# A decoder layer on one core: cross-attention's values projected in the first-norm stage instead of the sums stage

## The reference

```python
# self-attention: h = layernorm(x), scaled, quantised to 8 bits with a power-of-two scale
#   from max |h| over everything; q, k, v = quantised h @ w_qkv; 16 heads of 64
dots = fq_floor(q @ k.T * temp)              # scale again from a maximum over everything
attn = fq_floor(softmax(dots))               # needs the maximum over every row's sum
# cross-attention of x1 (the first block's result) to ctx (8, 512, 384)
k = ctx @ Wk + bk
v = ctx @ Wv + bv                            # 16 heads of 32
x = softmax(q @ k.T * scale) @ v @ Wo + bo
```

## Time and profile before

| | us |
|---|---|
| median of 3 runs | 2945.56 |
| lowest, highest | 2941.08, 2950.68 |
| profiled execution, its own time | 2947.2 |
| its span | 2945.4 |
| mean granted TensorE clock | 0.943 of 2.4 GHz |
| busy: TensorE, VectorE, ScalarE, GpSimd | 87%, 81%, 48%, 7% |

### The profile page before, as it was taken

The page is one execution under the profiler, slowest core; times in us unless marked ns, Lnnn a source line. Parts: engine busy times, 40 slices in busy tenths (PEclk is TensorE's granted clock), DMA queues, the critical chain, the costliest instruction groups (busy, mean ns, idle before and its releaser), DMA issues.

```text
span 2945.4 us, 43234 instructions
## 1 busy us (share of the span) xinstructions
PE 2549.4 (87%) x13176; PEld 995.6 (34%) x13176; DVE 2387.9 (81%) x4130; ACT 1403.5 (48%) x2456; POOL 217.9 (7%) x210
## 2 busy tenths in 40 slices
PE   3299899969999957777769799999999999999997
PEld 3244322212222224444335222222223444444443
DVE  7889499999999969999889589988897755555554
ACT  2200233318998989999523155555555322221211
POOL 0000233310111110000000000111100000000000
PEclk7599999969998979999989899999999999999999
DMA  8342222214454543443216633443355510000000
GB/s 320 109 184 93 90 105 101 94 65 158 164 180 150 164 144 113 128 125 114 72 43 200 152 84 102 115 110 103 101 169 197 197 72 29 29 29 28 29 29 29
DMA packets 197749, 332.90 MB, mean 113 GB/s; under 512 B 32504, under 2 KB 118520, under 8 KB 187248
## 3 DMA queue, kind: packets, MB, share of 16 engines
q1 hardware_dynamic: 193312, 314.51, 33.2%
q10 hardware_dynamic: 4304, 16.78, 1.5%
HBM read 200.70 MB, written 130.51 MB: 112 GB/s over the span
## 4 chain that ended last, share of the span: by engine, by line
PE 53%; DVE 21%; issue 15%; ACT 7%; DMA 2%; DVEq 1%; SPq 0%; POOLq 0%; POOL 0%; ACTq 0%
PE bank L1068 9%; PE bank L1234 7%; PE bank L1223 7%; ACT arena L1329 6%; DVE stats L1516 6%; PE bank L1024 4%; DVE arena L1797 4%; PE bank L1032 4%; PE bank L1008 4%; PE bank L1122 3%; DVE arena L1812 3%; PE bank L915 2%; PE bank L923 1%; PE bank L1040 1%; PE bank L983 1%
## 5 line engine op out<-in xcount | busy, mean ns | idle before, releaser
L1516 DVE TENSOR_REDUCE stats<-bank 128x1024 f32 (+1 forms) x352 | 406.4, 1216 | 54.8 <-PE bank L892 32.4
L1329 ACT ACTIVATE arena<-arena 128x512 bf16<-128x512 int8 x512 | 361.4, 713 | 72.9 <-DVE arena L1733 72.8
L1750 DVE CUSTOM_DVE_ANT_0 arena<-bank,arena,fac 128x512 int8<-128x512 f32 x512 | 355.8, 740 | 20.7 <-PE bank L915 20.7
L1917 DVE TENSOR_REDUCE arena<-bank 128x2 f32<-128x1024 f32 x256 | 312.5, 1223 | 52.1 <-PE bank L1024 36.4
L1422 ACT ACTIVATE arena<-bank 128x1024 f32<-128x1024 f32 x256 | 248.0, 1022 | 189.4 <-PE bank L1040 189.4
L1354 ACT ACTIVATE arena<-arena 128x512 f32<-128x512 int8 x512 | 323.7, 774 | 14.6 <-DMA arena<-dq_scr 14.6
L1492 ACT ACTIVATE arena<-bank,bf_s,fac 128x512 f32<-128x512 f32 x128 | 99.5, 778 | 434.1 <-PE bank L1226 434.1
L1307 ACT ACTIVATE arena<-bank,floor_c,fac 128x1024 int8<-128x1024 f32 x96 | 115.6, 1204 | 355.2 <-PE bank L855 304.6
L1068 PE MATMUL bank<-arena 128*32 128x512 f32 x2048 | 270.0, 604 | 0.0
L855 PE MATMUL bank<-arena 128*128 128x512 bf16 x1024 | 245.4, 384 | 26.3 <-DMA arena<-hq_scr 13.2
L1234 PE MATMUL bank<-arena 128*128 128x512 f16 x1024 | 245.6, 379 | 7.6 <-DVE arena L2114 7.1
(11 more groups left out here) (211 smaller groups left out, 3397.3 us busy)
## 6 DMA issues: line engine op xcount, KB each, us to landing
dq_scr<-arena SPq DMA_DIRECT2D x128, 256.0 KB, 2.1
arena<-dq_scr SPq DMA_DIRECT2D x128, 256.0 KB, 2.6
arena<-half_scr SPq DMA_DIRECT2D x256, 128.0 KB, 2.8
qkv_scr<-arena SPq DMA_DIRECT2D x8, 3072.0 KB, 9.7
arena<-in_x SPq DMA_DIRECT2D x16, 1024.0 KB, 8.4
arena<-qkv_scr SPq DMA_DIRECT2D x128, 128.0 KB, 2.4
half_scr<-arena SPq DMA_DIRECT2D x32, 512.0 KB, 4.0
x_scr<-arena SPq DMA_DIRECT2D x16, 1024.0 KB, 5.7
```

Of the source, the lines that this page charges most:

```text
L1329: last = A(e_dump[:, NT * (h % 2) + t, :], dq8[:, h % 4, t, :], ACT.Exp, bias=negm_b[:, par, c:c + 1], scale=exp_scale, accum_out=sum_b[:, ...
L1516: return V.tensor_reduce(dst, src, ax, ALU.max, apply_absolute_value=True)
L1750: V.tensor_tensor_reduce(dq8[:, s, t, :], bank[:, t, :], floor_row, fac[:, C_DOTS:C_DOTS + 1], -3.0e38, ALU.add, ALU.max, accum_out=ymax[: ...
L1917: V.tensor_reduce(mxX[:, mp, hs, 2 * u:2 * u + 2], bank[:, at:at + 2, :], AX.X, ALU.max).then_inc(S("sX_red"), 1)
```

## The change

Values are projected in the first norm. TensorE's `ctx_values(b)` follows `turn_z(b)`: 12 products in four banks; ctx and values go round banks 4 to 7 with one count (`kv_bank`, seven units a batch). ScalarE copies each block to `vI`, now two buffers (`values_kept`, after `h_out(b)`), GpSimd adds the bias in place, SyncE stores it. `cx` is a single buffer; Wv and bv are loaded at the start. VectorE's loop is now first_norm(b + 1), h_peak(b). In the sums stage only keys are left, one block each 16 tiles, a third of it after tiles 2, 7 and 12; VectorE evicts blocks 0 and 2, ScalarE 1 and 3. Scores go round six banks, and VectorE's loop over batches is written out.

```diff
@@ -267,9 +268,12 @@
 w8 = cB(I8, 4096)
-cx = cB(F32, 2, NT, DC)
+Wv_s = cB(F32, CC, D)
+bv_s = cB(F32, D)
+cx = cB(F32, NT, DC)
+vI = cB(F32, 2, D)
 KEEP_AT = ARENA - (24 + 8) * 256 - NB * CC * T
-assert cB.at <= KEEP_AT
+assert cB.at <= KEEP_AT, (cB.at, KEEP_AT)
 cxT = Carve(KEEP_AT)(F32, NB * CC, T)
@@ -445,11 +447,12 @@
     for b in range(NB):
+        if b + 1 < NB:
+            sp.wait_ge(S("kv_mm"), b * UNITS_V + CC)
+            load_ctx(b + 1)
         if b + 2 < NB:
             sp.wait_ge(S("z_turned"), b * NT + NT)
             load_x(b + 2)
-            sp.wait_ge(S("kv_mm"), b * CC + CC)
-            load_ctx(b + 2)
         sp.wait_ge(S("h_ready"), b * KC + KC)
@@ -457,6 +460,10 @@
                 load_h(n)
+        for t in range(NT):
+            sp.wait_ge(S("v_ready"), b * NT + t + 1)
+            sp.dma_start(v_scr[b * KC:b * KC + KC, :, t, :].rearrange("o p c -> p o c"),
+                         vI[:, t % 2, :].rearrange("p (o c) -> p o c", o=KC)).then_inc(S(f"v_stored{t % 2}"), 16)
     for n in (0, 1):
@@ -528,11 +530,9 @@
                 load_pair(b + 1, p)
-            if p == 2 and b:
+            if p == 1 and b:
                 store_k(b - 1)
-        store_v(b)
     store_k(NB - 1)
-    sp.wait_ge(S("v_stored"), 64 * NB)
     sp.wait_ge(S("k_stored"), 32 * NB)
@@ -767,7 +767,13 @@
     over_partitions(1, S_GAMMA, S_BETA + 1)
-    over_partitions(2, S_WQKV, S_WOUT + 1)
+    pool.wait_ge(S("wI_in"), 32)
+    for b in range(NB):
+        for t in range(NT):
+            pool.wait_ge(S("kv_evac"), b * UNITS_V + CC + t + 1)
+            nc.gpsimd.tensor_tensor(vI[:, t % 2, :], vI[:, t % 2, :], bv_s, ALU.add).then_inc(S("v_ready"), 1)
+        if b == 2:
+            over_partitions(2, S_WQKV, S_WOUT + 1)
     over_partitions(3, S_H, S_H + 1)
@@ -788,8 +794,8 @@
         for o in range(KC):
-            pool.wait_ge(S("kv_evac"), NB * CC + b * KC + o + 1)
-            if o == 0 and not is_batch(b, 0):
+            pool.wait_ge(S("t32_in"), b * KC + o + 1)
+            if o == 0 and b:
                 pool.wait_ge(S("k_stored"), b * 32)
@@ -833,20 +839,36 @@
+    def kv_bank(b, n):
+        before = b * UNITS_V + n - 4
+        if before >= 0:
+            pe.wait_ge(S("kv_evac"), before + 1)
+        return bank[:, 4 + (b * UNITS_V + n) % 4, :]
     def turn_ctx(b):
-        pe.wait_ge(S(f"c_in{b % 2}"), 16 * (b // 2) + 16)
+        pe.wait_ge(S("c_in"), 16 * b + 16)
         for k in range(CC):
-            n = b * CC + k
-            if n >= 4:
-                pe.wait_ge(S("kv_evac"), n - 3)
+            dst = kv_bank(b, k)
             for t in range(NT):
-                last = nc.tensor.transpose(bank[:, 4 + n % 4, P * t:P * t + P], cx[:, b % 2, t, P * k:P * k + P], ident[:, :])
+                last = nc.tensor.transpose(dst[:, P * t:P * t + P], cx[:, t, P * k:P * k + P], ident[:, :])
+            last.then_inc(S("kv_mm"), 1)
+    def ctx_values(b):
+        pe.wait_ge(S("kv_evac"), b * UNITS_V + CC)
+        for t in range(NT):
+            dst = kv_bank(b, CC + t)
+            for k in range(CC):
+                last = mm(dst, cxT[:, b * CC + k, P * t:P * t + P], Wv_s[:, k, :], start=k == 0, stop=k == CC - 1)
             last.then_inc(S("kv_mm"), 1)
     for b in range(NB):
         turn_ctx(b)
         turn_z(b)
+        if b == 0:
+            pe.wait_ge(S("wI_in"), 32)
+        ctx_values(b)
     pe.wait_ge(S("h_ready"), NB * KC)
-    pe.wait_ge(S("kv_evac"), NB * CC)
+    pe.wait_ge(S("kv_evac"), NB * UNITS_V)
@@ -914,18 +936,11 @@
-    def kv_step(b, p, k):
+    def key_step(b, o, k):
+        if k == 0 and b * KC + o >= 2:
+            pe.wait_ge(S("t32_in"), b * KC + o - 1)
+        last = mm(bank[:, 6 + o % 2, :], Wk_s[:, k, P * o:P * o + P], cxT[:, b * CC + k, :],
+                  start=k == 0, stop=k == CC - 1)
         if k == CC - 1:
@@ -934,11 +949,11 @@
             for t in range(NT):
-                pe.wait_ge(S("dq_done"), b * (H * NT) + NT * h + t + 1 + 4)
-                scores(h, t, bank[:, t, :]).then_inc(S("rs_tile"), 1)
-                n = NT * (h % 2) + t
-                if n in (1, 4, 7):
-                    kv_step(b, h // 2, n // 3)
+                n = b * (H * NT) + NT * h + t
+                pe.wait_ge(S("dq_done"), n + 3)
+                scores(h, t, bank[:, n % 6, :]).then_inc(S("rs_tile"), 1)
+                if n % 16 in (2, 7, 12):
+                    key_step(b, h // 4, n % 16 // 5)
     barrier(pe, 6)
@@ -1289,14 +1304,24 @@
     def ctx_turned_out(b):
-        for n in range(b * CC, b * CC + CC):
+        for k in range(CC):
+            n = b * UNITS_V + k
             act.wait_ge(S("kv_mm"), n + 1)
-            A(cxT[:, n, :], bank[:, 4 + n % 4, :], ACT.Copy).then_inc(S("kv_evac"), 1)
+            A(cxT[:, b * CC + k, :], bank[:, 4 + n % 4, :], ACT.Copy).then_inc(S("kv_evac"), 1)
+    def values_kept(b):
+        for t in range(NT):
+            n = b * UNITS_V + CC + t
+            act.wait_ge(S("kv_mm"), n + 1)
+            if b * NT + t >= 2:
+                act.wait_ge(S(f"v_stored{t % 2}"), 16 * (b * NT // 2 + t // 2))
+            A(vI[:, t % 2, :], bank[:, 4 + n % 4, :], ACT.Copy).then_inc(S("kv_evac"), 1)
     for b in range(NB):
         ctx_turned_out(b)
         if b == 0:
             act.wait_ge(S("b16_ready"), 1)
         h_out(b)
+        values_kept(b)
     barrier(act, 3)
@@ -1329,7 +1354,7 @@
             last.then_inc(S("sum_done"), 1)
-            if h % 4 == 3:
+            if h % 8 == 7:
                 keys_kept(b, h // 4)
@@ -1640,8 +1665,8 @@
     for b in range(NB - 1):
+        first_norm(b + 1)
         h_peak(b)
-        first_norm(b + 1)
         if b == 2:
@@ -1733,11 +1758,12 @@
-    def values_kept(b, t):
-        dve.wait_ge(S("kv_mm"), NB * CC + b * PAIRS + 2 * t + 1)
-        if t == 0 and not is_batch(b, 0):
-            dve.wait_ge(S("v_stored"), b * 64)
-        V.tensor_tensor(vI[:, t, :], bank[:, 4 + t % 2, :], bv_s, ALU.add).then_inc(S("v_ready"), 1)
+    def keys_kept(b, o):
+        dve.wait_ge(S("kv_mm"), NB * UNITS_V + b * KC + o + 1)
+        if b:
+            dve.wait_ge(S("split_done"), b * KC + o + 1 - KC)
+        V.tensor_scalar(t32[:, o, :], bank[:, 6 + o % 2, :], HALF, bk16[:, o:o + 1], ALU.mult, ALU.add
+                        ).then_inc(S("t32_in"), 1)
@@ -1747,7 +1773,7 @@
                 hold(dve)
-                V.tensor_tensor_reduce(dq8[:, s, t, :], bank[:, t, :], floor_row,
+                V.tensor_tensor_reduce(dq8[:, s, t, :], bank[:, (b * (H * NT) + NT * h + t) % 6, :], floor_row,
                                        fac[:, C_DOTS:C_DOTS + 1], -3.0e38, ALU.add, ALU.max,
@@ -1755,16 +1781,18 @@
                         pair_max(b - 1, 1 - par, PAIRS - 1, t)
-                if h % 4 == 3 and t == 0:
-                    values_kept(b, h // 4)
+                if h % 8 == 4 and t == 0:
+                    keys_kept(b, h // 4 - 1)
             if h == 5 and not is_batch(b, 0):
                 keep_rows(b - 1, 1 - par)
     dve.wait_ge(S("wI_in"), 16 * 4)
     V.tensor_scalar(bk16, bk16, HALF, None, ALU.mult).then_inc(S("b16_ready"), 1)
+    dve.wait_ge(S("b16_ready"), 2)
     dve.wait_ge(S("part_sized"), NB)
     link(amax(peak[:, S_WFC:S_WPROJ + 1], w_peak[:, :].rearrange("p (w n) -> p w n", w=2)))
     dve.sem_inc(peak_ready, 1)
-    through(dve, quantise)
+    for b in range(NB):
+        quantise(b, b % 2)
     for step in (0, 1):
         pair_max(NB - 1, 1, PAIRS - 1, step)
     dve.wait_ge(apeak_ready, 6)
```

More of the change, by code:

```diff
@@ L40 @@
 DUOS = QKV_UNITS // 2
+UNITS_V = CC + NT
 NEXT_AT = (7, 9, 11, 13)
@@ L100, in sem @@
             return ctx.enter_context(nc.semaphore(name))
-        ARENA = 196 * 1024 // 4
+        ARENA = 198 * 1024 // 4
         arena = sb("arena", [P, ARENA], F32)
@@ L432, in load_ctx @@
             def load_ctx(b):
-                sp.dma_start(cx[:, b % 2], tok(ctx_768[b])).then_inc(S(f"c_in{b % 2}"), 16)
+                sp.dma_start(cx, tok(ctx_768[b])).then_inc(S("c_in"), 16)
             load_ctx(0)
+            sp.dma_start(Wv_s, chunk(Wv)).then_inc(S("wI_in"), 16)
             load_x(0)
             load_x(1)
-            load_ctx(1)
+            sp.dma_start(bv_s, bv.rearrange("(a n) -> a n", a=1).broadcast_to([P, D])).then_inc(S("wI_in"), 16)
             def load_h(b):
@@ L479, in _ @@
             sp.wait_ge(S("hq_stored1"), 16 + 16 * NB // 2)
+            for n in (0, 1):
+                sp.wait_ge(S(f"v_stored{n}"), 32 * NB)
             barrier(sp, 3)
-            sp.dma_start(Wv_s, chunk(Wv)).then_inc(S("wI_in"), 16)
             sp.dma_start(Wk_s, chunk(Wk)).then_inc(S("wI_in"), 16)
@@ L512, in store_dq @@
                 sp.dma_start(dst, dq8[:, h % 4]).then_inc(S(f"dq_stored{h % 4}"), 16)
-            def store_v(b):
-                sp.wait_ge(S("v_ready"), b * NT + NT)
-                for o in range(KC):
-                    sp.dma_start(v_scr[b * KC + o], vI[:, :, P * o:P * o + P]).then_inc(S("v_stored"), 16)
```

(14 more changed lines are left out.)

8 lines of the change are left out of this document (2 added, 6 removed).

## The result

The changed kernel takes 2951.9 us in the median of 20 runs (2944.6 to 2956.9), the kernel before 2945.7 (20 runs, 2937.9 to 2953.3): ratio 1.0024, 95% interval 1.0016 to 1.0032. It is slower by a quarter of a per cent, where 2938 was forecast. So the two profiles differ by 1.7 us only, the medians by 6.

What follows compares the result with a forecast made beforehand. VectorE and ScalarE were taken as both full in the sums stage, VectorE as the long engine in the first norm. -17.6 (sums stage) + 10.4 (first norm) = -7.2 us: 2940.0 profiled, 2938 as median; range 2920 to 2960.

Steps and rivals of the forecast that it cites:

- the greatest gain: Sums stage: eight undisturbed batches at 373 us with all disturbance gone, against 399.6 before; 26.6 us at most.
- the range given: Sums stage: TensorE's granted clock forecast between 0.7 and 0.9 in the profile after.
- the 9 us for the time at the low clock: Sums stage: TensorE at low clock somewhat under half the stage loses 9 us, leaving a gain of 17.6.
- Rival A: Sums stage: TensorE keeps 2.4 GHz, idle never over half a microsecond; stage gains 26.6 us, kernel 2927; chance 0.24.
- The waits for key banks: Sums stage: key steps wait for the block two before; VectorE's evictions free, ScalarE's with two tiles (1.4 us) to spare.
- the last h at 139.5: First norm: the last batch's h ready at about 139.5 us instead of 143.0, 3.5 us earlier.
- its bounds of +3 to +20: First norm: about +10 us; +3 with fast adds and stores and no library change, +20 with TensorE's clock mostly low.
- the price of GpSimd's adds for VectorE: First norm: each bias add priced at 1.9 us on GpSimd, with no cost counted for VectorE.
- the landing of a store: First norm, two value buffers: a value store lands in 3.3 us in the median, up to 11.2.
- rival C: First norm: two value buffers set the pace; landings of 7 us give 20 us a batch, h(7) at 163, kernel 2959; chance 0.18.
- The tail: End of first norm: GpSimd's adds and library change put the next stage's first product at T + 24, T being h ready; +13.9 us.
- The swap: First norm: first_norm(b+1) before h_peak(b) fills gaps of at most about 15 us, most of it not to be had.

Runs made afterwards that it cites:

- before_swapped: The kernel before, with only VectorE's first_norm(b + 1) put ahead of h_peak(b); ratio 0.9977 to the kernel before.
- values_left_out: The changed kernel without the values' products, evictions and adds, one constant block stored in their place; one execution, 2926.4 us.
- no_bias: The changed kernel, two value buffers kept, without GpSimd's addition of the values' bias; stores follow ScalarE's eviction; ratio 0.9945 to the kernel before.
- before_written_out: The kernel before, with only VectorE's quantising loop of the sums stage written out for all eight batches; ratio 0.9977 to the kernel before.

## Why the prediction was wrong, point by point

It had the kernel 7 us faster; it is 6 us slower.

**The sums stage: right in kind, too small.** VectorE's pace and the 373 us of the greatest gain were right: 374.6, and in eight kernels between 374.6 and 376.9. The clock was in the range given (0.76). The term that fell is the 9 us for the time at the low clock. Its rate was right, 12.45 us a round against 12.4 worked out; wrong was to charge it to the stage. The spells end before a lead of six tiles is used up. Rival A's size came without its condition, the full clock: before TensorE's clock fell at 932 us its gaps from 924 us on had been 0.17 to 0.51 us, and no whole stall came first. The stage gained 24.2 in the profiles, 6.6 more than taken.

**The waits for key banks: right.** TensorE's key products (L942) have 0.0 us of idleness before them in that stage.

**The first norm's batches: the step that failed.** The prediction had the last h at 139.5; it was 157.3, 18 us off, and the first norm as a whole left its bounds of +3 to +20 with +29.9. What failed is the price of GpSimd's adds for VectorE. The prediction priced an add at 1.9 us for GpSimd, which was too much, and at nothing for VectorE; no step had them meet. They lengthened VectorE's steps by 11.7 us in the very stretch in which "With heavy VectorE batches ... this chain catches up", and in which VectorE is the bound. With the adds left out, the last h came 11.3 us earlier.

The second term is the landing of a store, 3.3 us in the median and up to 11.2 from a stage where the DMA engines had room (49% busy). The first four stores, while the weights load (332 GB/s over 24 to 50 us), took 10.8 in the median and 18.3 at most. They made h(1) 15.2 us late. VectorE felt less of it: its fourth batch starts 10.3 us after before_swapped's, and four buffers win back 5.2 of them (53.30 us). Most of the rest goes with the transfers, for values_left_out, which has the added stores and loads but no work on values, starts it at 52.46, 4.2 after before_swapped. That lateness is kept to the end: no_bias starts its fourth batch 8.2 us after before_swapped and has its last h 9.1 after. 10.3 + 11.7 - 1.6 (a shorter last hop) = 20.4 is the whole distance to before_swapped's last h, and the swap's own 6.1 bring it to 14.3.

This is rival C's place, and it had 0.18, but its condition was a landing of 7 us or more in every batch, and the median was 2.7. That its 163 lies near the 157 measured is in good part luck. Counted from the changed kernel's last h, four buffers win 6.4 to 7.3 us, leaving the adds out 11.3, both 12.5; without the adds the ring of two is worth 1.2 us, no more than traces of one kernel differ by.

**The tail: right.** T + 24 was worked out, T + 25.8 came: the second pair of adds at T + 12 (forecast: evicted at T + 11.1), 6.10 us before the reduction (5.96).

**The swap** was worth 6.1 us, more than the few microseconds left to it, and is in the 157.3 already.

**The sum.** 10.4 against 29.9 in the first norm, 17.6 against 24.2 in the sums stage, 4.0 us of gains around them that were put at nothing: 2940.0 + 19.5 - 6.6 - 4.0 = 2948.9, the profiled execution's own time. The median lies another 3 us higher; which stage has them no trace shows.

## What to carry to other kernels

Work moved to a stage where engines are "mostly idle" still passes through that stage's queues, buffers and shared memory interfaces: price a store by its landing in that stage, with what else loads there, and ask of each added GpSimd operation which VectorE operation runs beside it. A lateness that reaches the bounding engine before a stretch in which it is never idle is kept to the end of that stretch, and whatever lengthens its steps there comes on top. And a deeper lead between a producer and the bounding engine can be worth more than the work taken from the producer: with four banks the removal of the values cost 20 us, with six the stage was 13 us under before_written_out.
